# Dispatching tokens to experts with one fp32 product a block in place of a rounded part and its residual

## What is computed

```python
logits = jnp.einsum('bnd,de->bne', token_inputs, Wg)
gates = jax.nn.softmax(logits, axis=-1)
expert_idx = jnp.argmax(gates, axis=-1)
mask = jax.nn.one_hot(expert_idx, Wg.shape[1], dtype=dt)
gate = jnp.sum(gates * mask, axis=-1)
pos = jnp.cumsum(mask, axis=1) * mask - mask
keep = mask * (pos < capacity).astype(dt)
pos_oh = jax.nn.one_hot(pos.astype(jnp.int32), capacity, dtype=dt)
dispatch = keep[..., None] * pos_oh
...
expert_inputs = jnp.einsum('bnd,bnec->becd', token_inputs, dispatch)
h = jax.nn.gelu(jnp.einsum('becd,edh->bech', expert_inputs, W1))
expert_outputs = jnp.einsum('bech,ehd->becd', h, W2)
output = jnp.einsum('becd,bnec->bnd', expert_outputs, combine)
```

## Time and profile before

| | us |
|---|---|
| median of 3 runs (range) | 138.56 (138.42 to 139.27) |
| the profiled execution | 138.64 |
| its span, first to last instruction | 136.9 |

### The profile page before, as it was taken

One profiled execution on the slowest core, in us unless ns is written; L12 is line 12 of the kernel. 1 busy time (PEld: TensorE's weight loads), 2 busy tenths in 40 slices (PEclk: granted clock), 3 DMA queues, 4 the chain that ended last, 5 costly groups with the idle time before them and its releaser, 6 DMA issues.

```text
span 136.9 us, 2770 instructions
## 1 busy us (share of the span) xinstructions
PE 124.2 (91%) x1038; PEld 89.0 (65%) x1039; DVE 93.6 (68%) x304; ACT 79.4 (58%) x154; POOL 33.6 (25%) x54
## 2 busy tenths in 40 slices
PE   6999988999899998998978997699999999999950
PEld 2573843664664754754834943599999799987830
DVE  2797656996996996996997899974782041134751
ACT  1568383945855865765636678863694265315350
POOL 7633805005005005005000060027000065550000
PEclk9999999999999999999999999999999999999998
DMA  3989991000000000000000000000101201113115
GB/s 98 277 226 333 366 382 51 0 0 7 0 0 0 0 5 0 0 2 0 5 0 0 0 0 0 0 5 0 41 5 38 77 24 30 34 31 87 34 42 153
DMA packets 9197, 8.05 MB, mean 59 GB/s; under 512 B 601, under 2 KB 7028, under 8 KB 9184
## 3 DMA queue, kind: packets, MB, share of 16 engines
q1 hardware_dynamic: 8492, 7.28, 16.6%
q0 software_dynamic: 256, 0.40, 1.2%
q10 hardware_dynamic: 436, 0.20, 0.6%
HBM read 6.43 MB, written 1.57 MB: 58 GB/s over the span
## 4 chain that ended last, share of the span: by engine, by line
PE 71%; DVE 14%; ACT 9%; issue 3%; POOL 1%; ACTq 0%; DVEq 0%
PE ps L1302 11%; PE ps L1288 11%; PE ps L1144 6%; PE ps L1117 6%; PE ps L1136 5%; PE ps L1110 5%; PE ps L980 3%; PE ps L1314 3%; PE ps L1218 3%; ACT r_b L422 3%; PE ps L1063 3%; PE ps L1181 2%; PE ps L1093 2%; ACT z_b L436 2%; PE ps L1074 2%
## 5 line engine op out<-in xcount | busy, mean ns | idle before, releaser
L1144 PE MATMUL ps<-attn,VW 32*128 32x256 f32 x144 | 12.9, 426 | 3.5 <-DVE ps L712 2.0
L1288 PE MATMUL ps<-h,W_t 128*128 128x128 f32 x128 | 15.9, 279 | 0.0
L1288 PEld LDWEIGHTS ps<-h,W_t 128*128 128x128 f32 x128 | 15.0, 192 | 0.5 <-issue 0.3
L429 ACT ACTIVATE ps<-ps,half_b 128x512 f32<-128x512 f32 x12 | 7.9, 660 | 12.7 <-PE ps L1117 12.7
L1136 PE MATMUL ps<-h,whhT 128*128 128x256 f32 x48 | 13.7, 405 | 0.0
L1117 PE MATMUL ps<-h,whhT 128*128 128x256 f32 x48 | 13.3, 398 | 0.0
L346 POOL DMA_INDIRECT y_tok<-y_rows,row_of x8 | 8.3, 1034 | 18.9 <-DMA y_rows<-y_sb 14.1
L1144 PEld LDWEIGHTS ps<-attn,VW 32*128 32x128 f32 x144 | 5.6, 182 | 10.6 <-DVE ps L712 4.4
L1110 PE MATMUL ps<-h,whhT 128*128 128x256 f32 x48 | 11.7, 384 | 0.0
L422 ACT ACTIVATE r_b<-ps,half_b 128x512 f32<-128x512 f32 x12 | 7.6, 684 | 7.1 <-PE ps L1144 7.1
L712 DVE SCALAR_TENSOR_TENSOR ps<-r_b,ps 128x512 f32<-128x512 f32 x12 | 7.8, 693 | 5.1 <-ACT r_b L422 5.1
(11 more groups left out here) (168 smaller groups left out, 255.2 us busy)
## 6 DMA issues: line engine op xcount, KB each, us to landing
W_t<-in_L_ffn_W_dram SPq DMA_DIRECT2D x1, 2048.0 KB, 9.6
x_tok<-in_x_dram SPq DMA_DIRECT2D x4, 256.0 KB, 3.9
out_dram<-h SPq DMA_DIRECT2D x4, 256.0 KB, 2.3
y_rows<-y_sb SPq DMA_DIRECT2D x4, 128.0 KB, 1.8
n_b<-in_L_xattn_gru_whh_dram SPq DMA_DIRECT2D x1, 192.0 KB, 4.1
n_b<-in_L_xattn_gru_wih_dram SPq DMA_DIRECT2D x1, 192.0 KB, 3.5
y_tok<-y_rows,row_of POOLq DMA_INDIRECT x8, 3.7
n_b<-in_ctx_dram ACTq DMA_DIRECT2D x1, 64.0 KB, 2.9
```

The lines of the kernel that those rows point to most:

```text
L1144: last = mm(to[:, hf, :], VW[g][p:p + M, gate * P:(gate + 1) * P], attn[g][p:p + M, :], start=False, stop=True, skip_group_check=True)
L1288: last = mm(hid_bank[e][:, j * BG * CAP:(j + 1) * BG * CAP], W1_t[:, ex_, j * P:(j + 1) * P], rhs, start=True, stop=True)
```

## The change

The residual and the rounded copy disappear: the buffers x_hi and x_lo, the helpers x_high (ScalarE) and x_low (VectorE), their eight calls and their semaphores. The one-hot tiles have the type float32 instead of float32r. dispatch(b) multiplies xln, block by block, 4 products a batch instead of 8, each as soon as its one-hot tile and its normalized block are there. The filling products ahead of dispatch(0) are 10 instead of 12.

```diff
-        x_hi = sb("x_hi", [P, B * C, D], f32r)
-        x_lo = sb("x_lo", [P, B * C, D], f32r)
-        disp = sb("disp", [P, 2, C, N], f32r)
+        disp = sb("disp", [P, 2, C, N])
...
-            def x_high(b):
-
-                cs = slice(b * C, (b + 1) * C)
-                act.wait_ge(x2ln, (b + 1) * C)
-                nc.scalar.activation(x_hi[:, cs, :], xln[:, cs, :], ACT.Copy).then_inc(xhi, 1)
-
...
             x2_norm(0)
-            x_high(0)
             x2_norm(1)
-            x_high(1)
             gate_exp(0)
...
             x2_norm(2)
             gelu(2)
-            x_high(2)
             x2_norm(3)
-            x_high(3)
             y_out(1)
...
-            def x_low(b):
-
-                cs = slice(b * C, (b + 1) * C)
-                dve.wait_ge(xhi, b + 1)
-                v.tensor_tensor(x_lo[:, cs, :], xln[:, cs, :], x_hi[:, cs, :].bitcast(f32),
-                                ALU.subtract).then_inc(xlv, 1)
-
...
             x2_shift(1)
-            x_low(0)
             dispatch_hot(1)
             scale_logits(0)
-            x_low(1)
             weigh_n(g, 1, t)
...
             dispatch_hot(2)
-            x_low(2)
             dispatch_hot(3)
-            x_low(3)
             scale_logits(1)
...
-                for part in (x_hi, x_lo):
-                    pe.wait_ge(xhi if part is x_hi else xlv, b + 1)
-                    for c in range(C):
-                        if part is x_hi:
-                            pe.wait_ge(dsp, b * C + c + 1)
-                        last = mm(disp_bank[b][:, :], part[:, b * C + c, :], disp[:, b % 2, c, :],
-                                  start=(c == 0 and part is x_hi), stop=(c == C - 1 and part is x_lo))
+                for c in range(C):
+                    n = b * C + c
+                    pe.wait_ge(dsp, n + 1)
+                    pe.wait_ge(x2ln, n + 1)
+                    last = mm(disp_bank[b][:, :], xln[:, n, :], disp[:, b % 2, c, :], start=(c == 0), stop=(c == C - 1))
                 last.then_inc(xeP, 1)
...
             positions(0)
-            keep_clock(12, to=7)
+            keep_clock(10, to=7)
             dispatch(0)
             dispatch(1)
```

More of the change, by code:

```diff
@@ L222, in slot_attention_and_switch_ffn @@
         S = [{k: sem(f"{k}_{'AB'[g]}") for k in names} for g in range(NG)]
-        x2T, x2P, x2st, x2mv, x2rs, x2nm, x2ln, x2c, xhi, xlv = (
-            sem(n) for n in ("x2T", "x2P", "x2st", "x2mv", "x2rs", "x2nm", "x2ln", "x2c", "xhi", "xlv"))
+        x2T, x2P, x2st, x2mv, x2rs, x2nm, x2ln, x2c = (
+            sem(n) for n in ("x2T", "x2P", "x2st", "x2mv", "x2rs", "x2nm", "x2ln", "x2c"))
         lgP, lmx, dl, gl, lx, ls, gt, fi, fm, mk, posP, pl = (
```

## The result

| | before | after |
|---|---|---|
| median, runs | 138.87 us of 4 (138.42 to 139.27) | 143.14 us of 4 (142.50 to 143.49) |
| the profiled execution | 138.64 us | 142.98 us |
| its span | 136.9 us | 141.2 us |

The ratio is 1.0314, 95% interval 1.0288 to 1.0339: the kernel became slower by 4.3 us (4.27 between the medians, 4.36 by the ratio), against +4.10 predicted. Some executions run slower at a lower granted clock of TensorE, and the ratios leave them out; here these are two of e4's four.

The account below looks back on a forecast made before the run. TensorE (PE) was taken as the bound, though the first stage's waits run over ScalarE and VectorE. First stage +0.93 and second stage +3.17 gave +4.10 us, forecast 142.6 us, range 141.8 to 143.6.

Parts of the forecast that it names:

- Price of an fp32 product: Dispatch products of 512 columns: two records of 0.433 us each, 0.866 us a block, against 0.47 us for the split block.
- one record: Rival, dispatch: an fp32 product of 512 columns has one record of 0.433 us; total -1.4, 137.2 us; 4%.
- open weight loads: Rival, dispatch: each fp32 product's two weight loads aren't hidden, 0.97 us a block, 144.3 us; 6%.
- Second stage: Dispatch of batches 2 and 3, bound by PE alone: 6.93 us in place of 3.76, +3.17 us.
- First stage: Dispatch of batches 0 and 1: PE's waits hide part; first expert product at 90.1 instead of 89.17, +0.93 us.
- The removed work: Copies and subtractions gone: 0 in the second stage; in the first, xT earlier but the dispatch's end 2 us behind it.
- The clock: Rival, first stage: two missing filling products let PE's clock fall; batch 1's products 3.5 us more, 146.1 us; 3%.
- The last rival: First stage is hidden and only the second pays, the eviction wait covered by other products: 141.7 us; 3%.

Follow-up runs that it names:

- e4: Changed kernel with one rounded product a block, residual's part left out, normalization writing the rounded tile: ratio 0.9801 against the kernel before (two runs); median of four 136.89 us.
- e2: Kernel before with fp32 products in the second stage only (batches 2 and 3), without their copies and subtractions, 12 filling products: 141.66 us, ratio 1.0233.
- e1: Kernel before with fp32 products in the first stage only (batches 0 and 1), 10 filling products: 139.62 us, ratio 1.0103.
- e6: Changed kernel with 12 filling products instead of 10: 143.17 us, ratio 1.0335 against the kernel before.
- e5: Changed kernel with the four rounded copies and four subtractions put back at their old places, unread: 142.60 us, ratio 1.0302 against the kernel before.
- e3: Changed kernel without the 10 filling products before the first dispatch: 143.13 us, ratio 1.0334 against the kernel before.
- e7: Kernel before with batch 0 alone in fp32, the rest split, 10 filling products, VectorE's work in another order: 137.99 us, ratio 0.9951.
- e8: e4 with 7 filling products added behind the first dispatch: 135.64 us, ratio 0.9770 against the kernel before.

## Why the prediction was right

- *Price of an fp32 product.* Two records, 0.433 us each, was carried on from narrower ones. 6.94 us for 16 give 0.434, and 0.08 us of the 6.94 is the slower first record; without it a record takes 0.429. The price of the narrow rows carried over to 512 columns, and the rivals with one record and with open weight loads fall on the record count and on the pace (x32, PEld 190 ns each under records of 0.43).
- *Second stage.* +3.17 predicted, +3.22 measured, in e2 alone as well. Nothing hid it. The 0.05 is what is left of two small errors: the first record is slower by 0.10 (697 ns against 593), a cost that the prediction put at the row products instead and took as unchanged, and the others take 0.429 each instead of 0.433, 0.06 less in all.
- *First stage.* Start of the dispatch predicted 82.3, found 82.36; evictions at 86.9 and 89.45, found 86.95 and 89.50; first expert product at 90.1, found 90.15. +0.93 predicted, +0.94 without what came in before the positions. e1 shows it alone. That the two agree to 0.01 is in part luck. From the dispatch's start to the next product the prediction counts 6.93 + 0.1 us, and the trace has 6.94. Its terms add up to 89.49 for the end of the dispatch, where it wrote 89.45; the trace has 82.36 + 7.11 = 89.47. The start came 0.06 us later than it said. It put the 0.1 down to the change from bf16 products; e6 shows 0.08, and only where PE had to wait.
- *The removed work.* Worth nothing: e5. xT early by 1.3 us, as forecast (87.3, found 87.23), and of no use.
- *The clock.* It did not fall, and in e3 it didn't without any filling there either.
- The last rival (first stage free) falls with e1.
- *What the sum lacked.* After the wait for the eviction the first 16 expert records take 2.05 us where they took 1.95 behind the transposes; this is the 0.10 between the stages. I had the new wait but no cost for the first record behind it. The other traces in which the first expert product waits for the eviction at full clock have the 2.05 there too (e1, e6, e7, e8), and e2, where it doesn't wait, has 1.95. It isn't a cost of waiting alone: in the kernel before the same kind of product takes 2.05 us behind the products L1302, which have another shape, with no idle time (PE's timeline of before). Why is open.

```profile
100.83 2.05 PE L1288 MATMUL ps<-h,W_t 128*128 128x128 f32 x16
```

The 4.10 predicted, with 0.10 here, 0.04 from before the positions, 0.05 in the second stage and 0.01 in the first, make the 4.30 that the stretches add up to.

## What to carry to other kernels

Splitting an fp32 operand into two rounded parts against an exact one-hot tile costs two records (0.455 us together for 512 columns), where one fp32 product costs two records of nearly twice the length (0.868). Where PE is the bound, this is worth the copies on other engines; where PE waits for those copies, fp32 costs less (0.94 us instead of 3.22 here), and for one batch, together with another order on VectorE, it even gained (e7). The choice belongs to each place and not to the kernel. Before counting on removed work of other engines, look at what is late next: here it was PE itself, by 2 us.

## What the runs showed of the hardware that I had not expected

The same kind of gap did not act alike. PE stood still for 2.33 us in e3, and the granted clock stayed at 1.00. In e4's profiled execution it stood still for 1.57 us; the clock was still 1.00 when PE began again (87.40 to 88.00) and then lay at 0.50 (88.25 to 91.25). What PE did ahead of the gap was different. In e3 it was busy for 1.95 of the 2.00 us from 78 to 80. In e4 its eight dispatch records came about 0.39 us apart within a batch, near the 0.40 us at which VectorE writes one-hot tiles, though such a record takes 0.227 us when its tiles are ready; a reader who goes by busy time (1.64 and 1.62 us for four) doesn't see it. Whether this stretch or the gap behind it let the clock fall isn't shown: e8 filled the gap alone, and the clock held.

The fall cost 1.6 us in the first expert products (3.64 against the 2.05 of e8), nearly as much as the second dispatch had saved (3.76 to 1.94 us). A change that makes PE's work shorter can so lose part of its gain to the clock.

A stretch of products that PE had to wait for also takes a little longer than one that follows at once: 0.08 us for the fp32 dispatch (7.11 against 7.03 in e6), 0.10 for the expert products (2.05 against 1.95).
